# A last expert layer rebuilt as one stage, and result tiles that rotate through four PSUM banks instead of two

## The chip, the cores and the metric

One core of a Trainium2 chip runs the whole program. The metric is the device time of one execution in microseconds (us). TensorE (PE) does the matmuls, VectorE (DVE) and ScalarE (ACT) work on tiles in SBUF or PSUM, GpSimd (POOL) does indirect transfers and a few adds, SyncE (SP) issues most DMAs. PSUM, where matmul results arrive, has eight banks here: `K.ps[:, 0..7, :]`.

## The reference, cut to what matters

A graph of 3125 nodes with 256 features and 50,000 edges passes four pairs of layers. Each pair is a graph layer and an expert layer, with a residual add after each. The change touches three of the four expert layers:

```python
# layer 0: eight dense experts, three matrices each, every node through every expert
h = relu(bn(x @ W1[e] + b1[e])); h = relu(bn(h @ W2[e] + b2[e])); y = h @ Wo[e] + bo[e]
x = x + sum_e w[e] * y_e

# layer 1: two experts are picked for the whole graph (256 -> 512 -> 256)
h = gelu(x @ W1[e] + b1[e]); out = sum_e w[e] * (h @ W2[e] + b2[e])

# layer 3: one expert (256 -> 1024 -> 256) for the nodes with the largest router weight
weights = xn @ wr + br                      # xn = layernorm(x), one number per node
_, idx = top_k(weights, N // 2)             # N = 3125: 1562
sel = idx[: N // 2 - 1]                     # the smallest of them is dropped
y[sel] = (gelu(xn[sel] @ w1 + b1) @ w2 + b2) * weights[sel]
x = x + y + xn
```

The kernel computes layer 3 for all nodes and multiplies the result with a gate: the weight where the node is among the selected, else 0. For the gate it needs each node's rank, the number of nodes that stand ahead of it. Equal weights are ordered by node number.

## The kernel before, in words

The nodes lie in SBUF as 25 tiles of 125 nodes (`NT = 25`, padded to 128 columns where they are matmul operands). `UN = 5` tiles make a chunk, so an expert goes over five chunks. Each engine runs its own instruction list; they meet only at semaphores. A block of a `Phase` is one stage: all engines enter it together and leave it together, and SP clears its semaphores afterwards. Inside a loop (`Fori`) the wait values are in registers: `hold(eng, sem, n)` waits until `sem >= n`, `ahead(eng, sem, n)` until `sem >= n + 1` (such semaphores are given one count at the start by `start`). Outside loops a wait has a constant.

**Dense experts (`dense_experts`, layer 0).** 8 experts x 5 chunks = 40 chunks. For each, PE does the first matrix in two halves of 320 columns into banks 0, 1 and 2, 3 (`ps_one`, L1540), the second matrix into banks 4 to 7 (L1548), and then the five result tiles (`u` = 0 to 4, L1556), which take turns in banks 2 and 3 (`ps_out`). DVE takes each tile out of its bank with a bias add (L1491, "take" below; it counts `s_bias`), and adds it, times the gate, to `x` (L1494, counts `s_add`). PE may write tile `u` for `u` from 2 when take `u - 2` is done, and may start the second half of the next chunk's first matrix when all five takes are done. Weights of two experts are in SBUF at a time; SP loads the next two when PE has finished all result tiles of the two before (L1463).

**Wide experts (`wide_experts`, layers 1 and 3).** Per chunk, PE does the first layer in `2 * HC` half blocks through banks 0 to 3 (L2130), ACT applies gelu to each (L2112), and after the last of them PE does the five result tiles (L2137), which take turns in banks 4 and 5; the wait for DVE is as above. In layer 1 (`HC = 4`, two experts, ten chunks) DVE does take and add as above (L2094, L2096). In layer 3 (`HC = 8`, one expert, five chunks) DVE has other work, handed in as `beside`.

**The last expert layer before** is four stages. `rank_rows`: DVE puts the 3125 weights on a diagonal (L2575), PE spreads them as a row over all partitions with 14 matmul instructions (L2562), ACT copies them out, DVE reads off each node's own value (L2582, L2583). `wide_experts` with `node_ranks` as `beside`: for each of the 25 tiles DVE runs two passes over 3125 columns, one for equal values with a smaller number (L2590), one for larger values, summed into the rank (L2592), and behind them the take of that tile into `K.acc` (L2088). `add_largest`: gate from the ranks, then three operations over all nodes, `y * gate`, `x + aux`, `x + y` (L2609 to L2613). `store`: two DMAs of 2.8 and 0.3 MB.

In the profile an f32 matmul stands as two records, so a tile of the last layer (8 matmuls) is 16 records, a chunk's first layer 64 and its five result tiles 80.

## Time and profile before

| | us |
|---|---|
| median of 3 runs | 7054.67 (7048.02 to 7060.27) |
| span of the profiled execution | 7015.3 |
| dense experts of layer 0, first to last of DVE's adds | 2447 to 3031 |
| wide experts of layer 1, loads to last add | 3873 to 4070 |
| last expert layer: rank setup | 6716.7 to 6735.7 |
| its loads, until PE starts | 6736.8 to 6746.0 |
| its five chunks, with the rank passes | 6746.0 to 6978.4 |
| gate and three adds | 6979.4 to 7000.2 |
| store and end | 7000.8 to 7015.3 |

The profile page gives no other time of the profiled execution than its span, from the first to the last instruction. What the measured time has beyond it, 39.4 us between this span and the median, lies around the program.

A timeline row gives start, length, engine, source line, operation and operands, and in brackets how long the engine was idle before it and what ended that. "PEld" is the weight load of a matmul, which runs ahead of it. "x64" after a row means that 64 such instructions were merged into it.

### The profile page before, as it was taken

How to read it: one execution, taken by the hardware profiler on the slowest of the kernel's cores; microseconds unless marked ns; L12 is line 12 of the kernel's file. 1: busy time of each engine (PE TensorE's matmuls, PEld its weight loads, DVE VectorE, ACT ScalarE, POOL GpSimd, SP SyncE). 2: the span in 40 equal slices, each digit the busy share in tenths (PEclk: the TensorE clock that was granted, in tenths of full speed). 3: DMA queues.
4: the chain of work that ended last, by engine and by line, in shares of the span. 5: the costliest groups of instructions: out<-in, count | busy, mean ns of one | idle time of the engine just before them, and what ended most of it. 6: DMA issues, size and time to landing. Idle time of an engine off the chain costs nothing. (4 is left out here: it accounts for less than half of the span.)

```text
span 7015.3 us, 73781 instructions
## 1 busy us (share of the span) xinstructions
PE 4991.8 (71%) x21189; PEld 3466.3 (49%) x21189; DVE 4512.7 (64%) x7271; ACT 2064.0 (29%) x3714; POOL 1454.6 (21%) x1466
## 2 busy tenths in 40 slices
PE   0110488888888599989688869579926777667976
PEld 0000244544444466668577648568823333336854
DVE  5994599947999522232398270301049999998867
ACT  0000011122111133322233223222227777763321
POOL 0677666603666100001000010110020000000000
PEclk9999998999999699989899989789968888888978
DMA  1332233454333400014341002256534444433200
GB/s 28 122 132 75 57 112 102 99 188 179 102 114 101 67 9 9 9 46 122 102 137 53 14 25 73 90 163 184 173 93 158 154 155 155 151 107 120 87 13 18
DMA packets 375829, 683.70 MB, mean 97 GB/s; under 512 B 90626, under 2 KB 302651, under 8 KB 367900
## 3 DMA queue, kind: packets, MB, share of 16 engines
q1 hardware_dynamic: 300236, 523.14, 22.7%
q0 software_dynamic: 75344, 157.40, 8.6%
q8 instruction: 136, 2.23, 0.1%
q14 instruction: 113, 0.93, 0.0%
HBM read 507.64 MB, written 172.62 MB: 97 GB/s over the span
## 5 line engine op out<-in xcount | busy, mean ns | idle before, releaser
L812 PE MATMUL ps<-sum_hot_cell,sum_hot_src 128*128 128x500 bf16 x2640 | 771.1, 398 | 323.0 <-DVE sum_hot_src L756 209.2
L734 POOL DMA_INDIRECT sum_rows_in<-rel_table,rel_row x880 | 841.6, 956 | 445.9 <-issue 236.0
L758 DVE TENSOR_SCALAR sum_hot_cell<-x_nodes 128x1500 bf16<-128x1500 f16 (+1 forms) x880 | 892.3, 1014 | 2.3 <-issue 2.3
L1938 PE MATMUL ps<-att_ring,acc 125*65 125x500 f32 x1000 | 602.0, 688 | 307.0 <-DVE att_ring L1759 306.9
L817 PE MATMUL ps<-sum_rows_in,sum_hot 128*128 128x256 f32 x1760 | 596.1, 417 | 56.6 <-issue 52.1
L1876 ACT ACTIVATE att_ring<-att_ring,att_src 125x625 f32<-125x625 f32 x750 | 555.4, 808 | 253.2 <-DVE att_ring L1734 154.2
L1946 PE MATMUL ps<-acc,att_ring 125*125 125x257 f32 x2500 | 557.2, 386 | 42.5 <-DVE att_ring L1759 42.5
L812 PEld LDWEIGHTS ps<-sum_hot_cell,sum_hot_src 128*128 128x128 bf16 x2640 | 268.7, 102 | 614.1 <-issue 420.3
L1946 PEld LDWEIGHTS ps<-acc,att_ring 125*125 125x125 f32 x2500 | 475.8, 191 | 121.1 <-DVE att_ring L1759 46.2
L1700 DVE CUSTOM_DVE_ANT_0 att_masks<-att_masks,aux 125x3125 bf16<-125x3125 bf16 x150 | 510.7, 3411 | 32.3 <-ACT aux L1822 19.2
L1759 DVE SCALAR_TENSOR_TENSOR att_ring<-att_ring,att_cell 125x3125 f32<-125x3125 f32 (+1 forms) x162 | 512.0, 3167 | 1.6 <-ACT att_ring L1876 1.3
L603 POOL DMA_INDIRECT rec_dram<-rec,addr x392 | 430.3, 1098 | 302.1 <-POOLq L116 178.3
L817 PEld LDWEIGHTS ps<-sum_rows_in,sum_hot 128*128 128x128 f32 x1760 | 321.5, 203 | 200.6 <-issue 104.1
L1834 ACT ACTIVATE att_ring<-att_rows,att_src 125x625 f32<-125x625 f32 x500 | 363.3, 803 | 0.7
L754 DVE TENSOR_SCALAR sum_hot<-row_f,slot_dst,slot_w 128x128 f32<-128x128 f32 x880 | 312.0, 355 | 71.3 <-remote 37.7
L1740 DVE TENSOR_TENSOR att_ring<-att_ring,att_rows 125x3125 f32<-125x3125 f32 (+1 forms) x104 | 341.4, 3286 | 11.6 <-ACT att_ring L1834 11.5
L776 ACT COPY acc<-ps 128x256 f32<-128x256 f32 x50 | 18.6, 372 | 1122.2 <-PE ps L817 840.3
L1940 PEld LDWEIGHTS ps<-att_ring,acc 125*65 125x65 f32 x1000 | 155.7, 156 | 352.4 <-issue 352.4
L914 PE MATMUL ps<-aux,sum_wide 125*125 125x256 f32 x1250 | 299.6, 387 | 16.3 <-ACT sum_wide L863 16.3
L1491 DVE TENSOR_TENSOR experts_y<-ps,experts_bo 128x256 f32<-128x256 f32 x200 | 84.1, 420 | 338.0 <-PE ps L1556 337.8
L1938 PEld LDWEIGHTS ps<-att_ring,acc 125*65 125x65 f32 x1000 | 137.0, 158 | 326.8 <-DVE att_ring L1759 326.8
L673 PE MATMUL ps<-ident,rel_xin 128*128 128x128 f32 x50 | 17.2, 448 | 385.3 <-DVE rel_xin L623 384.3
(446 smaller groups left out, 8580.1 us busy)
## 6 DMA issues: line engine op xcount, KB each, us to landing
att_cell<-cells SPq DMA_DIRECT2D x150, 781.2 KB, 4.7
att_masks<-masks SPq DMA_DIRECT2D x150, 762.9 KB
...
sum_cell<-cells SPq DMA_DIRECT2D x125, 156.2 KB, 5.4
sage_cell<-cells SPq DMA_DIRECT2D x125, 156.2 KB, 2.2
...
```

What stands on the lines that cost most here:

```text
L603: pool.indirect_dma_start(K.rec_dram, bass.IndirectOffsetOnAxis(addr[:, j:j + 1], 0), rec[:, j, :], None).then_inc(scattered[j % 2], 16)
L734: pool.indirect_dma_start(rows_in[:, b, u, :], None, table, bass.IndirectOffsetOnAxis(rows[:, k:k + 1], 0)).then_inc(gathered[b], 16)
L758: dve.tensor_scalar(hot_cell[:, b, u, :], K.columns[:, :, 0:CW], K.cell[:, k], None, ALU.is_equal).then_inc(s_hot, 1)
L812: pe.matmul(K.ps[:, bass.ds(side * 4 + j, 1), 0:BW].rearrange("p a n -> p (a n)"), hot_src[:, b, u, :], hot_cell[:, b, u, j * BW:(j + 1) * ...
L817: pe.matmul(K.ps[:, bass.ds(side * 4 + 3, 1), 0:D].rearrange("p a n -> p (a n)"), hot[:, b, u, :], rows_in[:, b, u, :], start=False, stop= ...
L1700: dve.tensor_tensor_reduce(out=masks[0:NPT, n % MB, 0:N], in0=masks[0:NPT, n % MB, 0:N], in1=srow[h][0:NPT, :], scale=1.0, scalar=-BIG, op ...
L1740: dve.tensor_tensor(here, here, rows[0:NPT, r % 2, 1, :].unsqueeze(1).to_broadcast([NPT, n, GW]), ALU.add).then_inc(s_w, n)
L1759: dve.scalar_tensor_tensor(out=here, in0=here, scalar=1.0, in1=cell[0:NPT, b % CB3, i * n * GW:(i + 1) * n * GW], op0=ALU.min, op1=ALU.mul ...
L1834: act.activation(ring[0:NPT, b % RB, u, :], rows[0:NPT, r % 2, 0, :], ACT.Relu, bias=src8[0:NPT, s, h:h + 1]).then_inc(s_z, 1)
L1876: act.activation(here, here, ACT.Exp, bias=src2[0:NPT, q * UN + u, h:h + 1]).then_inc(s_e, 1)
L1938: pe.matmul(K.ps[0:W, side, 0:BAND], node_rows[s][0:NPT, h, :], ring[0:NPT, b % RB, v, 0:BAND], start=s == 0, stop=s == NT - 1).then_inc(s ...
L1946: pe.matmul(K.ps[0:NPT, u, 0:W], ring[0:NPT, b % RB, v, u * NPT:(u + 1) * NPT], node_rows[s][0:NPT, h, :], start=s == 0, stop=s == NT - 1) ...
```

## The change

Three things are edited.

1. **Dense experts:** result tiles rotate through banks 2, 3, 0, 1, so tile 4 is in bank 2 again. PE waits within the tiles only before tile 4 (for take 0). But banks 0 and 1 are also where the next chunk's first matrix begins, so PE now also waits at the chunk's start, until take 3 of the chunk before is done. `s_bias` starts at 2 instead of 1, so that the value waited for is never 0.
2. **Wide experts:** result tiles rotate through banks 4 to 7; PE waits before tile 0 for all takes of the chunk before, and before tile 4 for take 0. The `beside` branch is gone.
3. **Last expert layer:** `last_expert` takes the place of `rank_rows`, `wide_experts`, `add_largest` and `store`. It is written out without loops. The weights are loaded while DVE starts; the first layer of chunk 0 goes ahead of the row matmuls. There is one rank pass per tile (larger values only), one of them before the takes of chunk 0 and eight before those of each of chunks 1 to 3. POOL adds `aux` to `x`, tile by tile. Before the result tiles of the last chunk, a short sequence of small operations on DVE and three matmuls handles equal values at the border, and PE waits for the gate, since these matmuls use the banks of the result tiles. Then DVE does gate and add of 20 tiles, and take and add of each of the last five. SP stores chunk by chunk.

The first places where rows move are TensorE's in the dense experts. The names are semaphores of that stage: `experts0_bias` is `s_bias`, `experts0_h1` and `experts0_h2` count ACT's results. Before, a chunk's body up to the second matrix, and then its result tiles:

```order
L1540 ISA [waits experts0_h1]
L1540 MATMUL ps<-xt_nodes,experts_w 128x320
L1540 ISA
L1540 MATMUL ps<-xt_nodes,experts_w 128x320 x3
L67 ISA
L1540 ISA [waits experts0_bias]
L1540 MATMUL ps<-xt_nodes,experts_w 128x320
L1540 ISA
L1540 MATMUL ps<-xt_nodes,experts_w 128x320 x3
```

The first matmul of the chunk has no wait for a take. Further on in the same list of TensorE come the result tiles 1, 2 and 3:

```order
L1556 MATMUL ps<-experts_wo,experts_h 128x256 [waits experts0_h2]
L1556 MATMUL ps<-experts_wo,experts_h 128x256
L67 REGISTER_ALU [waits experts0_h2]
L1556 MATMUL ps<-experts_wo,experts_h 128x256 [waits experts0_bias]
L1556 MATMUL ps<-experts_wo,experts_h 128x256
L67 REGISTER_ALU [waits experts0_h2]
L1556 MATMUL ps<-experts_wo,experts_h 128x256 [waits experts0_bias]
L1556 MATMUL ps<-experts_wo,experts_h 128x256
```

Each tile from the third on waits for a take. The same start of a chunk on TensorE after the change:

```order
L67 ISA [waits experts0_h1]
L1539 ISA [waits experts0_bias]
L1539 MATMUL ps<-xt_nodes,experts_w 128x320
L1539 ISA
L1539 MATMUL ps<-xt_nodes,experts_w 128x320 x3
L67 REGISTER_ALU
L1539 ISA [waits experts0_bias]
```

The wait now stands ahead of the first matmul too. And the result tiles 2, 3 and 4 on TensorE after the change:

```order
L1555 MATMUL ps<-experts_wo,experts_h 128x256 [waits experts0_h2]
L1555 MATMUL ps<-experts_wo,experts_h 128x256
L1555 MATMUL ps<-experts_wo,experts_h 128x256 [waits experts0_h2]
L1555 MATMUL ps<-experts_wo,experts_h 128x256
L67 REGISTER_ALU [waits experts0_h2]
L1555 MATMUL ps<-experts_wo,experts_h 128x256 [waits experts0_bias]
L1555 MATMUL ps<-experts_wo,experts_h 128x256
```

The waits for `experts0_bias` ahead of tiles 2 and 3 are gone, and one stands ahead of the chunk's first matmul.

VectorE in the last expert layer, before: one tile's passes (`found`) and its take (`acc`) in the loop over chunks.

```order
L2590 SCALAR_TENSOR_TENSOR found<-rank_rows,own_value,earlier 128x3125
L67 REGISTER_ALU
L2592 REGISTER_ALU
L2592 SCALAR_TENSOR_TENSOR found,rank<-rank_rows,own_value,found 128x3125
L67 REGISTER_ALU x2
L2088 ISA
L2088 TENSOR_TENSOR acc<-ps,ffn_b 128x256
```

Two passes stand ahead of each take. Then, on the same engine, the stage of the adds:

```order
L115 UNCONDITIONAL_BRANCH
L2605 UNCONDITIONAL_BRANCH
L2609 SCALAR_TENSOR_TENSOR res_gate<-rank,token_w 128x25
L2611 TENSOR_TENSOR acc<-acc,res_gate 128x25x256
L2612 TENSOR_TENSOR x_nodes<-x_nodes,aux 128x6400
L2613 TENSOR_TENSOR x_nodes<-x_nodes,acc 128x6400
```

It begins only when the loop has ended on all engines. VectorE after the change, in chunks 0 and 1:

```order
L2601 TENSOR_REDUCE ffn_value<-ffn_diag 128x25
L2608 SCALAR_TENSOR_TENSOR ffn_found,ffn_rank<-ffn_rows,ffn_value,ffn_ones_row 128x3125
L2616 TENSOR_TENSOR acc<-ps,ffn_b 128x256 x5
L2608 SCALAR_TENSOR_TENSOR ffn_found,ffn_rank<-ffn_rows,ffn_value,ffn_ones_row 128x3125 x8
L2616 TENSOR_TENSOR acc<-ps,ffn_b 128x256 x5
```

One pass per tile is left, in groups of eight ahead of five takes. Further on, the end of the gate and what follows it on VectorE:

```order
L2648 TENSOR_TENSOR ffn_tie_before<-ffn_tie_before,ffn_rank 128x25
L2649 SCALAR_TENSOR_TENSOR ffn_gate<-ffn_tie_before,token_w 128x25
L2622 SCALAR_TENSOR_TENSOR x_nodes<-acc,ffn_gate,x_nodes 128x256 x20
L2616 TENSOR_TENSOR acc<-ps,ffn_b 128x256
L2622 SCALAR_TENSOR_TENSOR x_nodes<-acc,ffn_gate,x_nodes 128x256
```

The gate with the adds stands in the same stage.

TensorE in the last expert layer after the change, chunk 0 and the begin of chunk 1:

```order
L2696 MATMUL ps<-xt_nodes,ffn_w 128x320 x32
L2685 MATMUL ps<-ffn_diag,ones 128x500 x6
L2685 MATMUL ps<-ffn_diag,ones 128x125
L2719 MATMUL ps<-ffn_w,ffn_h 128x256 x40
L2696 MATMUL ps<-xt_nodes,ffn_w 128x320 x32
```

The row matmuls stand behind the first layer of chunk 0, where before they had a stage of their own. And chunk 4 of TensorE:

```order
L2696 MATMUL ps<-xt_nodes,ffn_w 128x320 x32
L2707 MATMUL ps<-ident,ffn_best 128x128
L2709 MATMUL ps<-ffn_tie,before 128x25
L2710 MATMUL ps<-ffn_tie,ones 128x25
L2719 MATMUL ps<-ffn_w,ffn_h 128x256 x40
```

Three small matmuls stand between the two layers of the last chunk.

The diff, cut to its core (the removed functions are shown above by name; `largest_gates`, which nothing called, is removed too):

```diff
@@ dense_experts
-        ps_out = [K.ps[:, 2, 0:D], K.ps[:, 3, 0:D]]
+        ps_out = [K.ps[:, 2, 0:D], K.ps[:, 3, 0:D], K.ps[:, 0, 0:D], K.ps[:, 1, 0:D]]
...
-            start(dve, s_add, s_bias)
+            start(dve, s_add, s_bias, s_bias)
...
-                        ahead(dve, s_bias, n + u + 1)
+                        hold(dve, s_bias, n + u + 3)
...
                         for h in range(2):
-                            if h == 1:
-                                ahead(pe, s_bias, m)
+                            hold(pe, s_bias, m + (2 if h == 1 else 1))
...
-                            if u >= 2:
-                                ahead(pe, s_bias, m + u - 1)
+                            if u == 4:
+                                hold(pe, s_bias, m + 3)
@@ wide_experts
-        ps_out = [K.ps[:, 4 + i, 0:D] for i in range(2)]
+        ps_out = [K.ps[:, 4 + i, 0:D] for i in range(4)]
...
-                            ahead(pe, s_bias, m + u - 1 if u > 1 else m)
+                            ahead(pe, s_bias, m + 1 if u == 4 else m)
@@ last_expert, SyncE
+            sp.dma_start(w1[:, :, :], K.inp[w1_name].rearrange("(c p) n -> p c n", p=P)).then_inc(w1_in, 16)
+            with nc.allow_non_contiguous_dma(reason="biases by partitions"):
+                sp.dma_start(b1[:, :], K.inp[b1_name].rearrange("(c p) -> p c", p=P)).then_inc(b1_in, 16)
+            sp.dma_start(w2[:, :, :], K.inp[w2_name].rearrange("(c p) n -> p c n", p=P)).then_inc(w2_in, 16)
+            sp.dma_start(b2[:, :], K.inp[b2_name].partition_broadcast(P)).then_inc(b2_in, 16)
+            for g in range(NCH):
+                t = slice(g * UN, (g + 1) * UN)
+                sp.wait_ge(s_done, (g + 1) * UN)
+                sp.dma_start(rows_out[0:112, t], K.x[0:112, t, :]).then_inc(stored, 16)
+                sp.dma_start(rows_out[112:NPT, t], K.x[112:NPT, t, :]).then_inc(stored, 16)
@@ last_expert, GpSimd
+            for t in range(NT):
+                pool.tensor_tensor(K.x[:, t, :], K.x[:, t, :], K.aux[:, t, :], ALU.add).then_inc(s_own, 1)
@@ last_expert, VectorE
+            def count_above(t):
+                if t > 0:
+                    dve.wait_ge(s_rank, t)
+                dve.scalar_tensor_tensor(out=found[:, :], in0=rows[:, :], scalar=value[:, t:t + 1], in1=ones[:, :],
+                                         op0=ALU.is_gt, op1=ALU.mult, accum_out=rank[:, t:t + 1]).then_inc(s_rank, 1)
+            def take(t):
+                dve.wait_ge(s_out, t + 1)
+                dve.tensor_tensor(y[:, t, :], ps_out[t % UN % 4], b2[:, :], ALU.add).then_inc(s_y, 1)
+            def settle(t):
+                dve.wait_ge(s_own, t + 1)
+                dve.wait_ge(s_y, t + 1)
+                dve.scalar_tensor_tensor(out=K.x[:, t, :], in0=y[:, t, :], scalar=gate[:, t:t + 1], in1=K.x[:, t, :],
+                                         op0=ALU.mult, op1=ALU.add).then_inc(s_done, 1)
+            for g in range(NCH - 1):
+                for t in range(ranked, min(NT, ranked + (1 if g == 0 else 8))):
+                    count_above(t)
+                for t in range(g * UN, (g + 1) * UN):
+                    take(t)
+            link(dve.tensor_scalar(inside[:, :], rank[:, :], float(count), real[:, 0:1], ALU.is_lt, ALU.mult))
+            link(dve.scalar_tensor_tensor(out=tie[:, :], in0=rank[:, :], scalar=1.0, in1=inside[:, :], op0=ALU.add, op1=ALU.mult))
+            dve.tensor_reduce(best[:, :], tie[:, :], AX, ALU.max).then_inc(s_top, 1)
+            dve.wait_ge(s_tops, 1)
+            link(dve.tensor_reduce(high[:, :], ps_top, AX, ALU.max))
+            link(dve.tensor_scalar(high[:, :], high[:, :], -1.0, None, ALU.add))
+            dve.tensor_scalar(tie[:, :], rank[:, :], high[:, 0:1], real[:, 0:1], ALU.is_equal, ALU.mult).then_inc(s_tie, 1)
+            dve.wait_ge(s_ties, 2)
+            link(dve.tensor_copy(total[:, :], ps_total))
+            link(dve.tensor_tensor_scan(before[:, :], one[:, :], total[:, :], 0.0, ALU.mult, ALU.add))
+            link(dve.tensor_tensor(before[:, :], before[:, :], total[:, :], ALU.subtract))
+            link(dve.tensor_tensor(before[:, :], before[:, :], ps_before, ALU.add))
+            link(dve.tensor_tensor(before[:, :], before[:, :], tie[:, :], ALU.mult))
+            link(dve.tensor_tensor(before[:, :], before[:, :], rank[:, :], ALU.add))
+            dve.scalar_tensor_tensor(out=gate[:, :], in0=before[:, :], scalar=float(count), in1=K.token_w[:, :],
+                                     op0=ALU.is_lt, op1=ALU.mult).then_inc(s_gate, 1)
+            dve.wait_ge(s_gate, 1)
+            for t in range((NCH - 1) * UN):
+                settle(t)
+            for t in range((NCH - 1) * UN, NT):
+                take(t)
+                settle(t)
@@ last_expert, TensorE
+            pe.wait_ge(w1_in, 16)
+            for g in range(NCH):
...
+                if g == 0:
+                    for i in range(len(cuts)):
+                        rows_of(i)
+                    pe.wait_ge(s_rowed, len(cuts))
+                    pe.wait_ge(w2_in, 16)
+                if g == NCH - 1:
+                    pe.wait_ge(s_y, m)
+                    pe.wait_ge(s_top, 1)
+                    pe.matmul(ps_top, best[:, 0:1].to_broadcast([P, P]), K.ident[:, :], start=True, stop=True).then_inc(s_tops, 1)
+                    pe.wait_ge(s_tie, 1)
+                    pe.matmul(ps_before, K.before[:, :], tie[:, :], start=True, stop=True).then_inc(s_ties, 1)
+                    pe.matmul(ps_total, K.ones[:, :], tie[:, :], start=True, stop=True).then_inc(s_ties, 1)
+                    pe.wait_ge(s_gate, 1)
+                pe.wait_ge(s_h, n + HC * 2)
+                for u in range(UN):
+                    if u == 4:
+                        pe.wait_ge(s_y, m + 1)
+                    elif g > 0 and u == 0:
+                        pe.wait_ge(s_y, m)
+                    for hc in range(HC):
+                        mm = pe.matmul(ps_out[u % 4], h[:, hc, u * P:(u + 1) * P], w2[:, hc, :], start=hc == 0, stop=hc == HC - 1)
+                    mm.then_inc(s_out, 1)
```

## Rows read from the trace of the kernel before

**Rows 1.** The page: the span of the profiled execution.

```profile
span 7015.3 us, 73781 instructions
```

**Rows 2.** Timeline, TensorE, last expert layer. Columns: start us, us, engine, line, operation, count, idle before.

```profile
6746.02 18.94 PE L2130 MATMUL ps<-xt_nodes,ffn_w 128*128 x64 [17.89 <-DMA ffn_b<-in_L_ffn_b]
6766.02 10.60 PE L2137 MATMUL ps<-ffn_w,ffn_h 128*128 128x256 f32 x48 [1.05 <-ACT ffn_h L2112]
6778.48 3.69 PE L2137 MATMUL ps<-ffn_w,ffn_h 128*128 128x256 f32 x16 [1.87 <-DVE acc L2088]
6786.42 5.38 PE L2137 MATMUL ps<-ffn_w,ffn_h 128*128 128x256 f32 x16 [4.24 <-DVE acc L2088]
6791.63 17.39 PE L2130 MATMUL ps<-xt_nodes,ffn_w 128*128 x64
```

**Rows 3.** Groups by line, DVE, last expert layer. Last columns: busy us, mean ns, idle before.

```profile
L2590 DVE SCALAR_TENSOR_TENSOR found<-rank_rows,own_value,earlier 128x3125 bf16<-128x3125 f32 x25 | 86.7, 3469 | 11.3 <-DMA ffn_b<-in_L_ffn_b 10.5 <-issue 0.8
```

**Rows 4.** Timeline, DVE: a second rank pass, and the bias add behind it.

```profile
6950.25 3.48 DVE L2592 SCALAR_TENSOR_TENSOR found<-rank_rows,own_value,found 128x3125 bf16<-128x3125 f32 x1 [0.22 <-DVE found L2590]
6954.15 0.42 DVE L2088 TENSOR_TENSOR acc<-ps,ffn_b 128x256 f32 x1 [0.42 <-DVE found L2592]
```

**Rows 5.** Busy time and granted clock (PEclk) of two stretches: dense experts, last expert layer.

```profile
core 0: us, PE busy (x) PEld busy (x) DVE busy (x) ACT busy (x) POOL busy (x), PEclk, DMA share, GB/s
2446.00:2560.10 114.10, 110.46 (x421) 76.99 (x420) 33.97 (x81) 39.71 (x65) 0.00 (x0) 1.00 0.00 0
6786.42:6791.63 5.21, 5.21 (x16) 4.26 (x17) 4.99 (x2) 0.00 (x0) 0.00 (x0) 0.67 0.00 0
```

**Rows 6.** Timeline, from the rank setup to the loads of the last expert's weights.

```profile
6716.74 3.42 DVE L2575 TENSOR_TENSOR pick_diag<-ident,token_w 128x3125 f32<-128x3125 f32 x1 [1.56 <-PEq L116]
6725.24 0.19 PEld L2562 LDWEIGHTS ps<-pick_diag,ones 128*128 128x128 f32 x1 [0.36 <-issue]
6725.66 0.19 PEld L2562 LDWEIGHTS ps<-pick_diag,ones 128*128 128x128 f32 x1 [0.23 <-issue]
6736.77 0.37 SPq L2844 DMA_DIRECT2D ffn_w<-in_L_ffn_w  x1
```

**Rows 7.** One line, L2844: time from the issue of the load of w1 to its landing.

```profile
DMA to landing us min/median/max: 4.9/4.9/4.9
```

**Rows 8.** Timeline, the last of the three adds over all nodes.

```profile
6993.38 6.82 DVE L2613 TENSOR_TENSOR x_nodes<-x_nodes,acc 128x6400 f32<-128x6400 f32 x1
```

**Rows 9.** Timeline, dense experts, one chunk end, and the loads of the next two experts.

```profile
2560.03 0.42 DVE L1491 TENSOR_TENSOR experts_y<-ps,experts_bo 128x256 f32<-128x256 f32 x1 [7.72 <-PE ps L1556]
2562.54 0.42 DVE L1491 TENSOR_TENSOR experts_y<-ps,experts_bo 128x256 f32<-128x256 f32 x1
2563.07 0.73 PEld L1556 LDWEIGHTS ps<-experts_wo,experts_h 128*128 128x128 f32 x4 [0.53 <-issue]
2563.83 0.42 DVE L1491 TENSOR_TENSOR experts_y<-ps,experts_bo 128x256 f32<-128x256 f32 x1
2563.98 4.07 PEld L1540 LDWEIGHTS ps<-xt_nodes,experts_w 128*128 128x128 f32 x16 [0.18 <-issue]
2578.59 0.90 SPq L1463 DMA_DIRECT2D experts_w<-in_L_ffn_W  x2
```

**Rows 10.** Waits of the dense experts: us in total, times, longest us.

```profile
PE ps L1540 <- DMA experts_wo<-in_L_ffn_Wo: 19.5, 3, 6.7
PE ps L1556 <- DVE experts_y L1491: 6.8, 43, 0.2
```

**Rows 11.** Timeline, DVE: two small operations, the second waiting for the first by a constant.

```profile
2434.14 0.17 DVE L1481 TENSOR_TENSOR experts_cst<-experts_cst 128x16 f32<-128x16 f32 x1
2434.35 0.18 DVE L1482 TENSOR_TENSOR experts_cst<-experts_cst 128x16 f32<-128x16 f32 x1
```

**Rows 12.** Timeline, DVE, wide experts of the second network: a bias add.

```profile
3933.60 0.42 DVE L2094 TENSOR_TENSOR ffn_y<-ps,ffn_b 128x256 f32<-128x256 f32 x1 [0.45 <-PE ps L2137]
```

**Rows 13.** Groups by line, GpSimd: an add of one tile.

```profile
L1241 POOL TENSOR_TENSOR x_nodes<-x_nodes,sage_y 128x256 f32<-128x256 f32 x25 | 18.4, 735 | 767.5 <-ACT sage_y L1264 767.5
```

209 lines of the change are left out of this document (84 added, 125 removed).

## The prediction

> **What bounds the kernel now.** I read the page first, for the span [rows 1], then the timeline by engine of the places that the change touches, then the waits and the granted clock there. The reader is to see three things. In the last expert layer a chunk on TensorE is: first layer 17.39 (64 records), lag of the last gelu 1.05, three result tiles 10.60 (48 records, so 0.221 each), a stand of 1.87, a tile of 3.69, a stand of 4.24, and the last tile of 5.21 (6786.42 to 6791.63) [rows 2]. That is 44.05, of which 35.1 are matmuls at full pace. The two stands are for a take that sits in VectorE's queue behind two rank passes of 3.48 each [rows 2 to 4]. Around these chunks nothing overlaps: TensorE's first matmul comes at 6746.02, 29.3 after the setup began at 6716.74 [rows 2, 6]; after it come the adds, the last of which ends at 7000.20, and a store until 7015.3 [rows 1, 8]. From 6716.74 to the end it is 298.6 us. In the dense experts TensorE never stands long for VectorE, 43 times for 0.15, 6.8 in all, and three times for weights [rows 10]; the granted clock is 1.00 (2.4 GHz) [rows 5].
>
> **The last expert layer, step by step.** The new stage is a chain on TensorE, so I add it up from 6716.74.
> - Load of w1: 4.9 from issue to landing [rows 7]. SyncE enters a stage together with VectorE, so 0 is added for the issue. From below 4.9; from above 9.3, the time from the issue at 6736.77 to the first matmul when it waited for all four loads [rows 2, 6]. I take 5.0, since it now waits for w1 alone.
> - First layer of chunk 0: 19.0, as the chunk that began after a long idle time took (18.94) [rows 2].
> - Row matmuls: 14 records at 0.42 [rows 6], the last two short, 5.3, and 0.8 until ACT has copied the last piece: 6.1. Before, the setup was in front of everything; now the diagonal (3.42) and the memset run beside the load and the first layer, 24 us of cover. The reading of each node's value and the first pass (3.4 + 3.4 + 3.5) run beside chunk 0's result tiles.
> - Result tiles of five chunks: 80 records x 0.221 = 17.67, x 5 = 88.3 [rows 2].
> - First layers of chunks 1 to 4 with the gelu lag: (17.39 + 1.05) x 4 = 73.8 [rows 2].
> - Is VectorE in time? It has 8 passes and 5 takes in a chunk of 36.1. A pass costs 3.48 and a gap; in a loop, with waits in registers, 3.90 from start to start [rows 4], which makes 31.2, and with waits by constants, where a small operation of 0.17 is followed after 0.21 [rows 11], about 3.55, which makes 28.4. The take that frees bank 4 is wanted 18.4 + 14.1 = 32.5 after the chunk's begin; VectorE comes free 0.6 after that begin. So it is 0.3 to 3 early with the take, and the passes cost nothing. The 25 passes that go [rows 3] are worth what TensorE's stands were, 1.87 + 4.24 and the slow records behind them, five times, not their own 86.7. Were that cover gone, a chunk would cost 1 to 2 more (second rival).
> - The gate: behind chunk 4's first layer come a matmul, three small VectorE operations, two matmuls, seven small operations, with hand-offs. At 0.21 per small operation [rows 11], two records of 0.22 and four shorter for the matmuls, and about 0.12 per hand-off (take ends 2562.96, weight load starts 2563.07 [rows 9]), 4.1; less the gelu lag that is counted already, 3.0. From below 2, from above 8 (each operation 0.4). After 4.24 of idle time 16 records took 5.38 instead of 3.69, at a granted clock of 0.67 over that stretch, so part of it at 1.2 GHz [rows 2, 5]; the standing here is broken by small matmuls, so I take 1.2 of these 1.7. Together 4.2.
> - After the last matmul: hand-off 0.2, take 0.42, add 0.5: 1.2. The other 20 adds of 0.5 lie beside the last 17.7 of matmuls. They replace three operations of 6.8 each.
> - Store: it took 15.1 for 25 tiles [rows 1, 8]. Only the last five tiles' part is left behind the end; from below a fifth, 3; from above all, 15.1. The nearest row is the 1 MB load with 4.9 [rows 7], for 0.64 MB here, with the end of the program 1.3: 6.2.
> - GpSimd's 25 adds: 0.735 each [rows 13], 18.4, over by 6736, wanted by 6890. Should VectorE's diagonal be slowed beside them, 24 us cover it. Cost 0, at most the few us by which that cover could be missed.
>
> Sum: 5.0 + 19.0 + 6.1 + 88.3 + 73.8 + 4.2 + 1.2 + 6.2 = 203.8. Gain 298.6 - 203.8 = 94.8.
>
> **Dense experts.** VectorE's pace here is its own: take 0 starts at 2560.03, take 2 at 2562.54, take 3 at 2563.83 [rows 9], 1.26 per tile. A tile is 4 records on TensorE, 4 x 0.221 = 0.88 by the records of the same shape [rows 2]. Today PE is held to that pace by three short waits and then starts the next chunk at 2563.98 without one. Now it runs ahead through the tiles, 3 x (1.26 - 0.88) = 1.1 sooner, and then stands until take 3 is done: 2563.83 + 0.42 + 0.11 = 2564.36. That is 0.38 later than 2563.98. Nothing shortens VectorE's takes; its chain take, wait, add is as it was. So each chunk becomes longer by 0.38, not shorter. Bounds: 1.1 shorter, if the new wait did not bite; 0.38 + 1.26 = 1.6 longer, if PE came to wait for the next take. I take 0.38, which these rows give directly. 40 chunks have 39 borders; at three of them PE waits for weights [rows 10], whose load is issued behind the last result tile [rows 9], and there the 1.1 is a gain. 36 x 0.38 - 3 x 1.1 = 13.7 - 3.4 = 10.3 slower.
>
> The row on the clock in this stage says 1.00, though PE stands for about 0.15 before tiles 2, 3 and 4 [rows 5, 10]. The Trainium skill (page "TensorE: Matmul & The Clock Gate", section "A second HAM failure mode: psum-queue depth-cycling") says that cycling results through PSUM banks can make the engine idle so often between groups that its clock goes up and down. By the row it does not here; by the page it might with a longer stand per chunk, and the fourth rival is what that would do, worked out from rows.
>
> **Wide experts of layer 1.** VectorE waits for TensorE before each take there (0.45 [rows 12]), so the banks were never what was waited for. 0, between -1 and +1.
>
> **The forecast.** Net gain 94.8 - 10.3 = 84.5 against the profiled span: 7015.3 - 84.5 = 6930.8. The span is 39.4 under the median, and that part, around the program, stays: 7054.67 - 84.5 = 6970.2.
>
> **Rivals.**
> 1. *The dense wait does not bite and the four banks pay:* PE's 1.1 per chunk is kept, 36 + 3 borders, 43 faster instead of 10.3 slower, 6970 - 53 = 6917. For it: PE does wait for takes today. Against it: take 3's end at 2564.25 lies behind the point at which PE starts now, and the order shows the wait ahead of the first matmul.
> 2. *VectorE or the chain of the gate is late in the new stage:* passes at 3.9 with a take pushed behind PE's demand, 1 to 2 per chunk for three chunks, the gate at 8 instead of 4, weights at 9.3, more of the store: 5 + 4 + 4 + 4 = 17, so 6987. For it: 0.7 us is thin. Against it: constants instead of registers.
> 3. *VectorE's takes get slower in the dense experts:* the register operation that stood behind the add now stands between take and add. At 0.1 per tile, over the three tiles that the new wait counts, 36 x 0.3 = 11, so 6981. Against it: the take's own 0.42 can hide it, and the gap may shrink as well as grow.
> 4. *The stand at the dense chunk's start lowers the clock:* 1.7 per border as behind the 4.24 us wait [rows 2], 36 x 1.7 = 61, so 7031. Against it: after 1.87 of idle time the next 16 records took 3.69, no longer than at full clock, and the new stand is about 1.5.
> 5. *Slower than before:* the clock stays at its lower level (1.2 GHz) through the new stage, because in chunk 0 TensorE starts cold and later stands for rows, gate and takes. Five chunks have 35.1 of matmuls each, 175 in all; at half clock as much again, so 6970 + 175 = 7145. It decides from 84.5 / 35.1, when two and a half of the five chunks run slow. Against it: today the clock is back within one tile of 5.38 after a stand of 4.24, about the longest that I expect in the new stage, and the next 64 records take 17.39 [rows 2].
>
> **Chances.** Forecast 0.67, first rival 0.07, second 0.13, third 0.07, fourth 0.03, fifth 0.03. What a measurement of this kernel can tell from no change is about 0.2%, 14 us. Of the fifth, 0.02 are slower and 0.01 fall near two and a half slow chunks, which is no change; the rest, 0.97, is faster. The range: around the forecast 0.2 per dense border, 7 in all, and 8 for the terms of the stage (load, gate, store, each 3 to 5); these and the second and third rival make 6950 to 6990. The first, fourth and fifth rival lie outside, 0.13.
>
> **What would show it.** In the profile after: the last stage about 204 us from its first VectorE operation to the end; chunks there 36.1 apart; no wait of TensorE for a take within these chunks; one stand of about 4 before the last result tiles; first matmul about 5 after the stage's begin. In the dense experts chunks about 14.5 apart instead of 14.1, PE waiting for takes about 36 times, 1.3 to 1.6 each, and none at tile 4. The prediction is wrong if dense chunks are 13.1 apart (first rival), or if the last stage's chunks are over 37 apart (second), or a granted clock under 0.9 in either (fourth, fifth).

## The result, and the profile after

| | us |
|---|---|
| kernel before, median of 4 runs | 7051.35 (7047.19 to 7060.27) |
| kernel after, median of 4 runs | 6975.85 (6972.80 to 6978.99) |
| ratio, 95% interval | 0.989 (0.9876 to 0.9904) |

The change takes 75.5 us off; 84.5 off, to 6970, was predicted. The time lies in the stated range of 6950 to 6990, 5.7 us above the forecast. The dense experts became slower, as forecast, but by about 20 us where 10.3 was said.

The page after, its span; it answers to [rows 1]:

```profile
span 6977.3 us, 73057 instructions
```

TensorE in the new last stage (start, length, engine, line, operands, count, idle before), to hold against [rows 2]:

```profile
6778.84 20.49 PE L2696 MATMUL ps<-xt_nodes,ffn_w 128*128 128x320 f32 x64 [6.81 <-DMA ffn_w<-in_L_ffn_w]
...
6805.19 17.53 PE L2719 MATMUL ps<-ffn_w,ffn_h 128*128 128x256 f32 x80 [0.61 <-ACT ffn_rows L2673]
6822.56 17.39 PE L2696 MATMUL ps<-xt_nodes,ffn_w 128*128 128x320 f32 x64
6840.56 17.53 PE L2719 MATMUL ps<-ffn_w,ffn_h 128*128 128x256 f32 x80 [0.62 <-ACT ffn_h L2669]
...
6911.32 17.53 PE L2719 MATMUL ps<-ffn_w,ffn_h 128*128 128x256 f32 x80 [0.62 <-ACT ffn_h L2669]
6928.69 17.39 PE L2696 MATMUL ps<-xt_nodes,ffn_w 128*128 128x320 f32 x64
6945.92 0.38 PE L2707 MATMUL ps<-ident,ffn_best 128*128 128x128 f32 x2
6947.21 0.40 PE L2709 MATMUL ps<-ffn_tie,before 128*128 128x25 f32 x2 [0.91 <-DVE ffn_tie L2641]
...
6949.46 20.54 PE L2719 MATMUL ps<-ffn_w,ffn_h 128*128 128x256 f32 x80 [1.62 <-DVE ffn_gate L2649]
```

The five result tiles of a chunk are now one unbroken row of 80 records: no bracket names a take. Chunks follow each other after 35.37 (6805.19 to 6840.56), where they took 44 before. The one stand is that for the gate, 6945.92 to 6949.46, 3.54 with its small matmuls.

VectorE in the second chunk (chunk 1) and at the end, and SyncE's last store; they answer to [rows 4] and [rows 8]:

```profile
6844.20 3.48 DVE L2608 SCALAR_TENSOR_TENSOR ffn_found<-ffn_rows,ffn_value,ffn_ones_row 128x3125 bf16<-128x3125 f32 x1
...
6847.71 3.48 DVE L2608 SCALAR_TENSOR_TENSOR ffn_found<-ffn_rows,ffn_value,ffn_ones_row 128x3125 bf16<-128x3125 f32 x1
...
6851.11 1.08 DVE L2616 TENSOR_TENSOR acc<-ps,ffn_b 128x256 f32<-128x256 f32 x3
...
6970.57 0.49 DVE L2622 SCALAR_TENSOR_TENSOR x_nodes<-acc,ffn_gate,x_nodes 128x256 f32<-128x256 f32 x1
```

```profile
6971.08 0.32 SPq L2580 DMA_DIRECT2D out<-x_nodes  x1
```

Passes follow each other after 3.51, with waits by constants, where [rows 4] had 3.90 with registers. Take 0 of the chunk starts at 6851.11; PE needs bank 4 again for the fifth tile, four tiles (14.0) after 6840.56, at 6854.6. So VectorE is 3 us early: that is its cover.

The dense experts, a chunk border on TensorE, on the weight loads and on VectorE, to hold against [rows 9]:

```profile
2581.38 4.48 PE L1555 MATMUL ps<-experts_wo,experts_h 128*128 128x256 f32 x20
2587.43 4.57 PE L1539 MATMUL ps<-xt_nodes,experts_w 128*128 x16 [1.57 <-DVE experts_y L1491]
...
2602.19 4.57 PE L1539 MATMUL ps<-xt_nodes,experts_w 128*128 x16 [1.57 <-DVE experts_y L1491]
```

```profile
2587.42 2.72 PEld L1539 LDWEIGHTS ps<-xt_nodes,experts_w 128*128 128x128 f32 x11 [1.97 <-issue]
```

```profile
2582.84 0.42 DVE L1491 TENSOR_TENSOR experts_y<-ps,experts_bo 128x256 f32<-128x256 f32 x1 [8.33 <-PE ps L1555]
...
2586.31 0.48 DVE L1494 SCALAR_TENSOR_TENSOR x_nodes<-experts_y,gate,x_nodes 128x256 f32 x1 [0.54 <-DVE experts_y L1491]
2586.71 0.42 DVE L1491 TENSOR_TENSOR experts_y<-ps,experts_bo 128x256 f32<-128x256 f32 x1
```

The five tiles run free (20 records in 4.48) and then PE stands for take 3, which begins at 2586.71. The period is 14.76 where it was 14.12 to 14.20. The waits of this stage (in total, times, longest) and its granted clock, for [rows 10] and [rows 5]:

```profile
PE ps L1539 <- DVE experts_y L1491: 57.1, 36, 1.9
```

```profile
core 0: us, PE busy (x) PEld busy (x) DVE busy (x) ACT busy (x) POOL busy (x), PEclk, DMA share, GB/s
2592.00:2606.40 14.40, 12.83 (x52) 9.52 (x52) 4.19 (x10) 4.81 (x8) 0.00 (x0) 1.00 0.00 0
6778.80:6800.00 21.20, 21.16 (x67) 14.35 (x67) 2.47 (x3) 9.71 (x17) 15.23 (x23) 0.86 0.17 55
6949.40:6970.10 20.70, 20.54 (x80) 17.17 (x80) 11.62 (x30) 0.00 (x0) 0.00 (x0) 0.85 0.41 125
```

The waits number 36, as counted beforehand. Over a chunk with such a wait (the first stretch) the clock is 1.00 (2.4 GHz). The first layer of chunk 0 of the last stage had 0.86, the program's last result tiles 0.85.

Where the 75.5 come from: the last stage takes 203.5 (6773.79, VectorE's first operation there, to 6977.3) for 298.6, a gain of 95.1; the dense stage, first take to last add, 603.1 for 583.3, a loss of 19.8. That leaves 75.3.

The 95.1 of the last stage are, by its parts: 24.2 ahead of TensorE's first matmul (5.1 for 29.3), 31.5 from there to the end of its last (191.2 for 222.7), and 39.3 behind it (7.3 for 46.6). The 191.2 include 6.0 for the row matmuls and 3.5 for the gate, which the kernel before does outside its chunks. Counted there, the two ends give 54 and the chunks 41. The last matmul of the kernel before starts at 6968.3 and ends at 6968.7 (first and last start of this line of the kernel, in both stages that use it):

```profile
L2137 PE MATMUL ps<-ffn_w,ffn_h x800: 379/379/763, 3892.6 to 6968.3; 128*128 128x256 f32 x160
```

So more than half of the gain comes from work that stood alone at the two ends and now runs beside other work, and the rest from shorter chunks.

The spans of the two profiled executions differ by only 38.0. The rest lies in code that the change does not touch: the first take of the dense experts starts 32.4 later in the kernel after (2479.1 for 2446.7), and 5 more come between the two stages. A second profiled execution of the kernel before, `before_again` in the experiments, has a span of 7054.8, 39.5 longer than the first, and starts that take at 2472.1. Of the 39.5, 25.4 lie ahead of the take, 10.7 between the two stages and 3.5 in the last stage. So the execution that was profiled before the prediction was a short one, most of all in the first graph layer, and the difference of two spans is not the effect of a change.

### The profile page after: what moved, and what is told of

Its sections match the earlier page's. It is cut to its first block and busy times, and to the rows that moved or that the text cites. A ratio compares the mean times of both kernels' runs of the same rounds, so it can differ in the third digit from the quotient of the medians.

```text
span 6977.3 us, 73057 instructions
## 1 busy us (share of the span) xinstructions
PE 4947.7 (71%) x21195; PEld 3470.4 (50%) x21195; DVE 4407.1 (63%) x7280; ACT 2059.9 (30%) x3710; POOL 1477.3 (21%) x1491
## 5 line engine op out<-in xcount | busy, mean ns | idle before, releaser
L2587 POOL TENSOR_TENSOR x_nodes<-x_nodes,aux 128x256 f32<-128x256 f32 x25 | 20.2, 849 | 1560.3 <-POOLq L116 1560.3
```

## The experiments

Twelve runs in three groups, each group with the kernel before beside it on its chip. There the kernel before took 6937 (group 1), 7046 (group 2) and 6934 us (group 3). All statements go by differences or ratios within a group. The difference between the chips lies in the gathers of the first graph layer. Here is the kernel after in group 2, then in group 3 (the numbers behind the colon are the durations in ns, then the first and the last start):

```profile
L734 POOL DMA_INDIRECT sum_rows_in<-rel_table,rel_row x880: 943/949/1064, 790.1 to 2344.5; - x176
```

```profile
L734 POOL DMA_INDIRECT sum_rows_in<-rel_table,rel_row x880: 940/947/1032, 788.0 to 2214.0; - x176
```

That is 1554.4 and 1426.0, 128.4 apart, where the medians of this kernel are 127.4 apart. One gather takes as long on either chip (median 949 and 947 ns), so what differs is the time between them; why is not known.

### The two parts apart (group 1)

`dense_before` is the kernel after with the old `dense_experts`, `dense_alone` the kernel before with the new one. The diff between them in `dense_experts`:

```diff
-        ps_out = [K.ps[:, 2, 0:D], K.ps[:, 3, 0:D]]
+        ps_out = [K.ps[:, 2, 0:D], K.ps[:, 3, 0:D], K.ps[:, 0, 0:D], K.ps[:, 1, 0:D]]
...
-                            if h == 1:
-                                ahead(pe, s_bias, m)
+                            hold(pe, s_bias, m + (2 if h == 1 else 1))
...
-                            if u >= 2:
-                                ahead(pe, s_bias, m + u - 1)
+                            if u == 4:
+                                hold(pe, s_bias, m + 3)
```

> The kernel after with the dense experts as they were before (two result banks, PE waits for take 1 and take 3 of the chunk before at two places); the last stage is the new one. Theory (the dense experts' new chunk border costs 0.64 us, 36 times, less three entries at 1.1 = 19.8 us, as the starts of the takes stand in the two profiles): 19.8 us faster than the kernel after, about 6956, ratio to the kernel before 0.9866, and the chunks 14.13 us apart. Rival 1 (the border costs what the prediction said, 0.38, and the rest of the difference between the two profiles is of the execution): 10.3 us faster, 6966. Rival 2 (the dense experts cost nothing, the last stage alone gave 75): 6976.

> The kernel before with the new dense experts alone (four result banks, one wait for the last take at the head of a chunk); the last stage stays the old one. Theory: 19.8 us slower than the kernel before, ratio 1.0028, chunks 14.77 us apart, PE waiting 36 times for 1.4 to 1.6 us for VectorE. Rival 1 (0.38 a border): +10.3, ratio 1.0015. Rival 2 (nothing): 1.000.

`dense_alone`: 6955.95 for 6937.17, ratio 1.003 (1.0021 to 1.0039), 18.8 slower. The theory holds and rival 1 does not: the interval begins at 1.0021 (14.6 us), and 10.3 would be 1.0015. Its borders are 14.76 to 14.81 apart. The new result banks make the dense experts slower, by themselves.

`dense_before`: 6823.54, ratio 0.9837 (0.9823 to 0.985), 113.6 faster than the kernel before; 95 was expected. The profiles of the two runs say where the 130.1 between their spans (6952.0 and 6821.9) lie. The first take and the last add of the dense experts, in `dense_alone`, then in `dense_before`:

```profile
L1491 DVE TENSOR_TENSOR experts_y<-ps,experts_bo x200: 414/418/426, 2365.1 to 2971.7; 128x256 f32<-128x256 f32 x100
L1494 DVE SCALAR_TENSOR_TENSOR x_nodes<-experts_y,gate,x_nodes x200: 483/485/488, 2365.9 to 2972.6; 128x256 f32 x100
```

```profile
L1491 DVE TENSOR_TENSOR experts_y<-ps,experts_bo x200: 414/418/426, 2356.0 to 2939.6; 128x256 f32<-128x256 f32 x100
L1494 DVE SCALAR_TENSOR_TENSOR x_nodes<-experts_y,gate,x_nodes x200: 483/485/487, 2356.9 to 2940.5; 128x256 f32 x100
```

That is 607.5 and 584.5 us, 23.0 apart. From the last attention mask to the end it is 432.0 and 334.1, 97.9 apart. And 9.1 lie ahead of the first take (2365.1 for 2356.0), in the gathers, whose code is the same in both. By the same measure the last part gained 93.4 in the first pair of traces and 96.9 in group 2; from VectorE's first operation in the last stage to the end it is 95.1, 98.6 (group 2) and 97.9 (group 1). So the traces show a gain of 95 to 99 in the last stage, and not 113.6. In group 2 the gathers of the kernel before end 4 us earlier than those of the kernel after (2340.4 for 2344.5), not later. That a kernel with the old last stage is 9 us longer in the gathers on the chips of groups 1 and 3 is seen in one trace only. The times fit it (from group 2 to group 3 the kernel after is 127 us quicker, the kernel before 112), but why stays open, and it was not tried.

The kernel after itself, unchanged, in groups 2 and 3, and a trace of the kernel before:

> The kernel after, unchanged, timed beside the experiments. Where it stands on a chip on which the kernel before takes 6937 us is open: the kernel with the new last stage alone stood 113.6 us below the kernel before there and the one with the new dense experts alone 18.8 us above. If the two parts add, this one stands 94.8 us below (ratio 0.9863); if it is as in the first measurement, 75.5 us below (0.9892). The dense chunks 14.77 us apart, the last stage 200 to 204 us either way.

> The kernel before, unchanged, one look for its trace on this chip. Open: whether the two relation sums of the first graph layer (code that no kernel here changes) take about 1451 us, as in the kernel with the old last stage, or about 1442, as in the three with the new one. The first would say that some 9 us of the 113.6 are outside both changed parts. Dense chunks 14.15 apart, the old last part 298 to 300 us.

> The kernel after, unchanged, as the reference of the three kernels beside it: ratio to the kernel before 0.989 if the chip is like the one of the first measurement (7046 us for the kernel before), 0.986 to 0.987 if it is like the one on which the kernel before takes 6937 us and the parts add.

`after_again`: 6978.6 for 7045.8, ratio 0.9898 (0.988 to 0.9915). `after_third`: 6851.16 for 6933.76, 0.9883 (0.9868 to 0.9898). Both intervals contain 0.989. The 0.9863 that the two parts of group 1 add up to lies outside the first of them. By the medians the change took off 75.5, 67.2 and 82.6 in the three measurements. In the traces the two changed stages give 75.3 in the first pair and 75.5 in group 2 (98.6 less 23.1); what is left over lies in code that is the same in both. `before_again` took 7056.5 with a span of 7054.8. Its borders are 14.11 to 14.20 apart and its dense stage is 583.2 long; that of `after_again` and `after_third` is 606.3 and 607.4. The loss in the dense experts is thus 20 to 24 by the traces. These two traces are 3.2 and 4.3 longer than the first. Of that, 1.7 sits near the stage's entry: in four of the eight profiles with the new chunk head, these two among them, the second chunk took 16.47 and in the others 14.8, since its first 16 records took 6.26 and not 4.57. The granted clock over these records is 0.73 in `after_again` and 1.00 in the first trace. The rest lies where the weights of the next experts are waited for, and in the first chunk behind it.

### Which part of the border costs (groups 1 and 3)

Two kernels keep four banks and change what a chunk's head has to wait for. `banks_4_to_7` puts the result tiles into the banks of the second matrix and waits for the five takes ahead of that matrix:

```diff
-        ps_out = [K.ps[:, 2, 0:D], K.ps[:, 3, 0:D], K.ps[:, 0, 0:D], K.ps[:, 1, 0:D]]
+        ps_out = [K.ps[:, 4 + i, 0:D] for i in range(4)]
...
-                            hold(pe, s_bias, m + (2 if h == 1 else 1))
...
+                            if h == 0:
+                                ahead(pe, s_bias, m)
```

> The kernel after with one thing changed in the dense experts: the four result tiles go to banks 4 to 7, which the hidden tile of the next chunk's first half does not use, so the wait for the takes moves from the head of the chunk to the head of its second half, some 4 us later. Theory (the 1.4 to 1.6 us that PE stands at a chunk's head is all there is of VectorE in the period; without it PE runs 4 x 0.07 + 8.9 + 4.1 = about 13.04 us a chunk): no wait for a take, chunks about 13.0 us apart, the dense stage about 541 us where it was 603, the kernel about 6914, ratio 0.980. Rival (ScalarE's gelu or the hidden tiles of the second half become the wait in its place, as VectorE's takes at 12 x 0.43 plus four passes of 128x512 do not shrink): PE waits at the second half instead, chunks 13.8 to 14.5, 6940 to 6970.

`split_wait` waits at the head for take 2 only, at the second block for take 3:

```diff
-                            hold(pe, s_bias, m + (2 if h == 1 else 1))
                             for oc in range(DC):
+                                if h == 0 or oc == 0:
+                                    hold(pe, s_bias, m + (3 if h == 1 else 1 + oc))
```

> The kernel after, same four banks, but the head of a chunk waits only for the take that frees bank 0, and the second block of the half for the take that frees bank 1. Theory: PE stands 0.2 to 0.4 us instead of 1.57 at a border, chunks 13.3 to 13.5 apart, the kernel about 6930, ratio 0.983. Rival (takes end at their own pace and PE stands again at the second block): 14.1 to 14.5 a chunk, 6955 to 6970.

`banks_4_to_7`: 6782.56, ratio 0.9774 (0.9761 to 0.9788), 155 faster than the kernel before. TensorE in it:

```profile
2406.97 4.48 PE L1556 MATMUL ps<-experts_wo,experts_h 128*128 128x256 f32 x20
2411.28 4.47 PE L1538 MATMUL ps<-xt_nodes,experts_w 128*128 x16
2415.59 4.47 PE L1548 MATMUL ps<-experts_h,experts_w 128*128 128x320 f32 x16
2419.90 4.48 PE L1556 MATMUL ps<-experts_wo,experts_h 128*128 128x256 f32 x20
```

There is no bracket in a whole chunk, and the next chunk follows after 12.93; the dense stage takes 538.6 (the theory said about 13.0 and 541). The period is 1.84 shorter than in the kernel after, of which the bracket there names 1.57, and 1.2 shorter than in the kernel before, which also lost time to VectorE, in its three short waits. So all that VectorE cost in a period was its waits, and it was not the number of banks but which ones: banks 0 and 1 are the first that the next chunk writes. With banks 4 to 7 the takes have the 4.3 us of the next chunk's first matrix to end. The rival (a new wait 4 us later) did not come. The weights of the next experts still arrive late three times, 20.3 in all for the 19.5 of [rows 10].

`split_wait`: 6814.76, ratio 0.9821 (0.9808 to 0.9835). Chunks 13.82 to 13.92 apart; the theory had 13.3 to 13.5, the rival 14.1 to 14.5. Both were wrong, and the rows say why. Here are the weight loads, then the takes that they wait for:

```profile
2468.89 0.84 PEld L1540 LDWEIGHTS ps<-xt_nodes,experts_w 128*128 128x128 f32 x4 [0.61 <-issue]
2470.08 0.84 PEld L1540 LDWEIGHTS ps<-xt_nodes,experts_w 128*128 128x128 f32 x4 [0.35 <-issue]
2471.51 1.91 PEld L1540 LDWEIGHTS ps<-xt_nodes,experts_w 128*128 128x128 f32 x8 [0.59 <-issue]
```

```profile
2468.18 0.42 DVE L1491 TENSOR_TENSOR experts_y<-ps,experts_bo 128x256 f32<-128x256 f32 x1
...
2469.55 0.42 DVE L1491 TENSOR_TENSOR experts_y<-ps,experts_bo 128x256 f32<-128x256 f32 x1
...
2470.81 0.42 DVE L1491 TENSOR_TENSOR experts_y<-ps,experts_bo 128x256 f32<-128x256 f32 x1
```

The third stand is for take 4, which frees bank 2 for the second half. The theory had left it out. The period is now VectorE's five takes, 5.56 from take 0's start to take 4's end (2465.67 to 2471.23), 0.28 until PE goes on, and 8.03 until the next take 0: 13.87.

The same rows hold the second finding. From a take's end to the weight load that waited for it, it is 2468.60 to 2468.89 = 0.29, 2469.97 to 2470.08 = 0.11, and 2471.23 to 2471.51 = 0.28. In the order of PE's instructions in this kernel the second wait is on the matmul itself, the first and third on an address operation (ISA) ahead of it:

```
L1540 ISA [waits experts0_bias]
L1540 MATMUL ps<-xt_nodes,experts_w 128x320
L1540 ISA
L1540 MATMUL ps<-xt_nodes,experts_w 128x320
L67 REGISTER_ALU
L1540 MATMUL ps<-xt_nodes,experts_w 128x320 [waits experts0_bias]
L1540 MATMUL ps<-xt_nodes,experts_w 128x320
L67 REGISTER_ALU
L1540 ISA [waits experts0_bias]
```

These are readings of two kernels, this one and the kernel after; no run changed the form of a wait and nothing else.

### The last stage (groups 2 and 3)

Is the cover of the rank passes real, and how thick? Each pass is done twice:

```diff
+                for again in range(2):
...
+                    dve.scalar_tensor_tensor(out=found[:, :], in0=rows[:, :], scalar=value[:, t:t + 1], in1=ones[:, :],
```

> The kernel after with each rank pass of the last stage done twice (25 more of 3.52 us, same result). Theory (the passes cost nothing only because VectorE has 36 us per chunk of which it uses some 27 in chunks 1 to 3, and the passes for the next four or eight tiles stand ahead of the takes): 16 passes take 56.3 us in each of the chunks 1 and 2 and 3, which is more than PE's 35.4, so PE waits for the first take some 20 to 24 us in each, chunk 0 gains 3.5: 65 to 75 us slower than the kernel after. Rival 1 (the passes are on the path as they stand): 25 x 3.52 = 88 us slower. Rival 2 (they run wholly aside): no change.

7058.2 for the 6978.6 of `after_again`: 79.6 slower, between theory and rival 1. One chunk of it, TensorE and then VectorE:

```profile
6838.19 14.08 PE L2722 MATMUL ps<-ffn_w,ffn_h 128*128 128x256 f32 x64 [0.62 <-ACT ffn_h L2672]
6877.35 5.51 PE L2722 MATMUL ps<-ffn_w,ffn_h 128*128 128x256 f32 x16 [25.08 <-DVE acc L2619]
...
6900.71 4.58 PE L2722 MATMUL ps<-ffn_w,ffn_h 128*128 128x256 f32 x20 [0.62 <-ACT ffn_h L2672]
```

```profile
6876.88 1.41 DVE L2619 TENSOR_TENSOR acc<-ps,ffn_b 128x256 f32<-128x256 f32 x4
6882.90 0.42 DVE L2619 TENSOR_TENSOR acc<-ps,ffn_b 128x256 f32<-128x256 f32 x1 [4.61 <-PE ps L2722]
6883.24 3.47 DVE L2611 SCALAR_TENSOR_TENSOR ffn_found<-ffn_rows,ffn_value,ffn_ones_row 128x3125 bf16<-128x3125 f32 x1
```

Eight passes more are 28.1, and PE stands 25.08 for the take behind them: the cover was 3.0. The 16 records after the stand take 5.51 where 3.5 is their time at full clock, 2.0 more. Together 27.1, and the period is 62.52 (6838.19 to 6900.71) for 35.38. The theory had set 56.3 of passes against the whole of 35.4; but from take 0 to the next pass (6876.88 to 6883.24) VectorE waits for the fifth tile, 6.4 that lie in series with the passes. From one chunk's result tiles to the next, this kernel is 0.5, 27.1, 28.3 and 27.2 longer than `after_again`, and its last tiles are 3.0 shorter: 80.2, for 79.6 measured. So the passes are free under a cover of 3 us per chunk, and what goes beyond it is paid in full and with slow records on top. With every pass done twice, as many passes as the kernel before has, nothing of the gain is left: 7058.2 for the 7045.8 of the kernel before, ratio 1.0018 (1.0008 to 1.0028). The rebuilt stage pays only together with the pass that was taken out, at least with eight tiles' passes ahead of five takes.

Are four banks what gives this cover? The last layer with two:

```diff
-                    if u == 4:
-                        pe.wait_ge(s_y, m + 1)
+                    if u >= 2:
+                        pe.wait_ge(s_y, m + u - 1)
...
-                        mm = pe.matmul(ps_out[u % 4], ...
+                        mm = pe.matmul(ps_out[u % 2], ...
```

> The kernel after with two result banks in the last expert layer where it has four. Theory (four banks are what lets PE finish a chunk's first four result tiles while VectorE still counts ranks; with two, tile 2 waits for take 0, which stands behind the chunk's passes): in chunks 1 and 2 the eight passes end 10.5 us after the first result tile starts and tile 2 would start after 7.0, so PE stands 3.5 to 4 us in each of chunks 0 to 3, and every later tile follows a take: 15 us slower than the kernel after. Rival (the passes have slack, the takes are 0.42 us each): no change, within 2 us.

6866.81 for the 6851.16 of `after_third`: 15.7 slower, for the theory's 15. The four runs of each lie apart (6862.8 to 6870.3 for 6849.1 to 6856.5), which rules the rival out. The waits for takes (in total, times, longest), and the result tiles of one chunk:

```profile
PE ps L2719 <- DVE acc L2616: 15.2, 4, 3.9
```

```profile
6710.71 7.17 PE L2719 MATMUL ps<-ffn_w,ffn_h 128*128 128x256 f32 x32 [0.62 <-ACT ffn_h L2669]
6721.73 12.13 PE L2719 MATMUL ps<-ffn_w,ffn_h 128*128 128x256 f32 x48 [3.85 <-DVE acc L2616]
```

The waits are there, four times, where the theory put them. The theory left out what follows: these 48 records take 12.13 and not 10.6, at a granted clock of 0.85 (6721.7 to 6732.4). With it the last stage is 20.6 longer than in `after_third` (221.5 for 200.9). That the medians say 15.7, close to the theory, is thus in part chance.

The store of all rows at the end, in place of five:

```diff
-            for g in range(NCH):
-                t = slice(g * UN, (g + 1) * UN)
-                sp.wait_ge(s_done, (g + 1) * UN)
+            sp.wait_ge(s_done, NT)
```

> The kernel after with the output stored by one transfer after the last addition, where it stores each chunk's rows as they are done. Theory (the stores of chunks 0 to 3 lie beside the last chunk's result tiles; 3.2 MB at what a whole store of the kernel before took leaves some 14 to 15 us at the end where there are 6.2 now): 8 to 9 us slower. Rival (what ends the program is the fixed cost of a transfer, not its size): no change.

6861.77: 10.6 slower. Its runs (6856.1 to 6865.8) only just touch those of `after_third`, and the trace gives the size. The issue of the store:

```profile
6838.20 0.36 SPq L2578 DMA_DIRECT2D out<-x_nodes  x1
```

From there to the end of the span (6854.4) it is 16.2, for the 6.2 of the kernel after (6971.08 to 6977.3): 10.0 longer.

The gate's three matmuls inside the last chunk's first layer:

```diff
+                    if g == NCH - 1 and hc == 1:
+                        pe.wait_ge(s_y, m)
+                        pe.wait_ge(s_top, 1)
+                        pe.matmul(ps_top, ...
+                    if g == NCH - 1 and hc == 3:
+                        pe.wait_ge(s_tie, 1)
+                        pe.matmul(ps_before, ...
+                        pe.matmul(ps_total, ...
```

> The kernel after with the three small matmuls that the last gate needs (the top and the tie counts) placed inside the last chunk's first layer, after its second and its fourth tile, and not behind it; same results. Theory: the stand of 3.5 us ahead of the last result tiles goes, and with it the 3.0 us of slow clock in them (20.5 us where the others take 17.5): 6 us faster than the kernel after. Rival (the wait for VectorE only moves into the first layer, since the gate's chain of small operations is what ends late): 0 to 2 us faster, PE standing inside the first layer instead.

6968.7, ratio 0.9886 (0.9869 to 0.9902) beside 0.9898 (0.988 to 0.9915) for `after_again`. The intervals overlap, so the times do not settle it; the trace does, at its place:

```profile
6908.63 17.53 PE L2721 MATMUL ps<-ffn_w,ffn_h 128*128 128x256 f32 x80 [0.62 <-ACT ffn_h L2669]
...
6930.31 0.38 PE L2702 MATMUL ps<-ident,ffn_best 128*128 128x128 f32 x2
...
6934.84 0.30 PE L2705 MATMUL ps<-ffn_tie,before 128*128 128x25 f32 x2
...
6944.73 17.50 PE L2721 MATMUL ps<-ffn_w,ffn_h 128*128 128x256 f32 x80 [0.66 <-issue]
```

The last tiles start 36.10 after those of the chunk before (38.14 in the kernel after) and take 17.50 (20.54): 5.1 less. The small matmuls wait for nothing. Of the 5.1, the 2.04 of the stand are what the edit gives each time. The 3.04 of slow records are what it gives at most, since behind the same stand they were 0 and 1.7 in other profiles.

Both mended, banks 4 to 7 and the gate inside:

> The kernel after with the result tiles of the dense experts in banks 4 to 7 (no wait at a chunk's head) and with the gate's three small matmuls inside the last chunk's first layer. Theory: the two gains add, 36 x 1.84 us = 66 less two to three for the entries in the dense stage and 5 in the last chunk: 68 to 72 us faster than the kernel after, about 6908 where that takes 6978. Rival (what the dense stage gives is taken back by its weights, which then come late: PE waited 20.3 us for them three times in the run with banks 4 to 7): 55 to 62.

6782.27, ratio 0.9781 (0.9768 to 0.9794): 68.9 faster than `after_third`, as the theory had it, and 151.5 faster than the kernel before. In the traces the dense stage is 69.1 shorter (2353.7 to 2892.0), which the rival's 55 to 62 does not allow, and the last stage 3.9. This is the best version that was run, with `banks_4_to_7`, from which the times do not tell it apart (0.9774).

## Why the prediction was right, and where it was not

**The last stage: right in its mechanism and in its sum.** 203.5 for 203.8. Measured, with the prediction's value in brackets: load 5.1 (5.0), first layer of chunk 0 20.3 (19.0), row matmuls 6.0 (6.1), result tiles at full clock 87.0 (88.3), first layers of chunks 1 to 4 with the lag 72.0 (73.8), gate with slow records 5.8 (4.2), end 1.1 (1.2), store 6.2 (6.2). That the sum is right to 0.3 is luck: terms that are off by 1.3 to 1.8 in either direction cancel. The lag of the last gelu is 0.62 and not the 1.05 of [rows 2]. The gate was right as a stand (2.8 beyond the lag, for 3.0) and off in what follows: the slow records behind it cost 3.0, not 1.2. Taking off part of the 1.7 because small matmuls break the stand had no row behind it. Nor is 3.0 a fixed number: after the same 1.62 of waiting, the 80 records took 20.5 (kernel after, `after_again`), 19.2 (`after_third`) and 17.5 (`two_passes`).

**The passes: right.** They cost nothing. The cover is 3 us, the upper end of "0.3 to 3 early", as the rows of passes with waits by constants had it. `two_passes` shows it, and `two_banks_last` that it is there only with four banks. What the change gained from them is the stands they caused and not their own 86.7: a chunk shrank from 44 to 35.4.

**The dense experts: right in sign and place, wrong in size.** The step was "2563.83 + 0.42 + 0.11 = 2564.36", 0.38 per border; it is 0.63. The failed term is the 0.11 for the hand-off. It was read at a result tile [rows 9], where the wait is on the matmul. At a chunk's head the wait is on the address operation ahead of it, and there it is 0.29 (2587.13 to 2587.42). The order of instructions shown ahead of the prediction had that form. `split_wait` has both forms in one kernel. That is 0.18 of the missing 0.25; the other 0.07 is take 0 to take 3, 3.87 for 3.80, with one gap of 0.54 among those of 0.43. 36 x 0.63 - 3 x 1.1 = 19.4, and 19.8 was measured in the first pair, 18.8 by time in `dense_alone`; the other traces have 23 to 24. In the first pair the 3 x 1.1 hold: with the weights late, the step to the next pair of experts takes 19.4 to 19.7 where it took 20.5 to 21.0. In `after_again` and `after_third` it takes 19.8 to 20.4, so less of the 1.1 is left.

**Wide experts of layer 1: right.** First gelu to last add is 185.3 before (3884.1 to 4069.4) and 184.6 after (3934.9 to 4119.5).

**"The span is 39.4 under the median, and that part, around the program, stays": wrong.** The profiled execution of the kernel after took 6978.99 with a span of 6977.3, and that of `before_again` 7056.52 with 7054.8. What lies around the program is 1.7. The 39.4 was an execution that was quicker than the timed ones, mostly in the first graph layer. It did no harm, since the difference was put on the median and none of the changed stages lies there.

**The rivals.** The first (the wait does not bite) fell with the 36 waits. The second fell: neither passes nor gate were late, though the gate with its slow records took 1.6 of the 4 it was given there. The third (a register operation between take and add) gave 0.07 per border for its 0.3, if the one longer gap is its doing, which no run shows. The fourth fell: the clock is 1.00 over a chunk with the stand of 1.57. The Trainium skill ("TensorE: Matmul & The Clock Gate", "A second HAM failure mode: psum-queue depth-cycling") tells of a bf16 kernel with 512 columns whose clock goes up and down while it cycles through PSUM banks; with the f32 tiles of 256 and 320 columns here the row shows no such thing. The fifth fell: in the last stage only the first layer of chunk 0 (0.86) and the last tiles (0.85) ran under 1.00. None of the stated signs of being wrong came: dense chunks are 14.77 apart, the last stage's 35.4, and the clock is 0.98 over the dense stage (2484 to 3082) and 0.97 over the last stage's matmuls (6778.8 to 6970.1).

The gain was forecast 9.0 too large (84.5 for 75.5), and nearly all of that is the dense experts' term, 19.8 for 10.3. That the time itself is off by only 5.7 is luck: with a fourth run the median of the kernel before fell by 3.3, from 7054.67 to 7051.35.
